# Matmul products beside two attentions, cut into runs of 12 and placed from tables; fewer transfers that clear the maxima rows

## The chip, the cores and the metric

One NeuronCore of a Trainium2 chip runs the whole program. The metric is the device time of one execution in microseconds, as the median of several runs. The engines work side by side, each through its own list of instructions in order: TensorE (PE, matmuls, with its weight loads shown as PEld), VectorE (DVE), ScalarE (ACT), GpSimd (POOL), and SyncE (SP), whose queue issues nearly all of the transfers. Engines wait for each other on semaphores.

## The reference, cut to what matters

Two transformer layers on `x` of shape (8, 1024, 256), 8 being the batch, all in float32.

```python
x = x + attn0(layernorm(x), Mq, Mk, Mv)         # 8 heads, softmax(q k^T / 8) over 1024 keys
x = x + fp4_ffn(layernorm(x), w_gate, w_up, w_down)   # blockwise FP4 quantized SwiGLU, 704 wide
x = x + attn1(layernorm(x), w_qkv, ...)          # 16 heads of 16, q and k normalised, softmax(q k^T)
x = x + moe_lora(layernorm(x), W, b, R, A, B)    # base product, top 2 of 8 experts, rank 16
```

Products with float16 operands are made three times over (high by high, high by low, low by high halves), so that the sum is as exact as float32 needs.

## The kernel before, in words

The work of a batch element (below: a batch) is done in tiles of 128 rows, 8 tiles a batch. Its two attentions have 64 steps each. A step of attention 0 (`attn0`) is one block of scores in `pS` (16 matmuls, L459, half of `pS` each), a maximum on DVE (L1239), an exponential of 1,024 columns on ACT (L914) with its row sums, a reciprocal of the sums on DVE (L1256), a scaling of the values on POOL (L1726), and the values' matmuls into `pV` (L560), some steps later. A step of attention 1 (`attn1`) is four score matmuls of 512 columns (L650), four exponentials of 512 columns (L953), and eight value matmuls (L690), one step later. Its scores take no maximum: two rows of the queries' operand that would carry maxima are filled with zeros. These are the maxima rows of the title. They get other contents only if a flag, computed from the data, asks for the general path.

Everything else is done beside these two attentions. The program has phases. In phase x of a period the steps of `attn1` for batch i-1 run beside the feed-forward part of batch i (`ffn`: gate and up products of 352 columns, down products of 256) and the first products of batch i+1 (`ln0`, `ln0_values`). In phase y the steps of `attn0` for batch i+1 run beside its later projections, the mixture part of batch i-1 (`moe_proj`, `moe_rt`, `moe`) and the heads of batch i (`heads_qkv`, `heads_T`). Batches 0 and 1 and the last batch have special cases at both ends of the program.

Which instruction follows which on an engine is fixed when the program is built. Each part is a generator (a lane) that yields a place, a number on a scale on which attention step n stands at n, and then issues its next piece. `weave` always lets the lane with the lowest place go on:

```python
while at:
    first = min(at, key=lambda x: x[:2])
    place = next(first[2], None)
```

Places come from small formulas, one set for all five engines, such as `ffn_at(t) = .5 + 6.75 * t` and `qkv_at(t)`, with fixed offsets per engine. A piece on PE is a whole product, or half of a long one: 24 matmuls of 352 columns for a gate or an up product, 36 of 256 for half of a down product, 48 of 256 for a projection (`project`) or for a pair of value tiles. `mm3` issues 12 matmuls at once: three combinations of halves, each as four matmuls on 32 of the 128 columns of weights.

```python
def mm3(dst, w, m, start=True, stop=True):
    by_columns(dst, w[0], m[0], start, False)
    by_columns(dst, w[0], m[1], False, False)
    return by_columns(dst, w[1], m[0], False, stop)
```

All these products share a ring of three banks, `pR`. `take` hands them out in turn, and waits on PE until the use before of the same bank has been read (`r_free`). `pS` and `pV` belong to the attentions.

The SP queue issues in its own woven order: `fill` (L1958), which copies the operands of `attn0`; `halves` (L1962), a transposing transfer of normalised rows; `put` (L2072), which writes the heads to a scratch tensor `scr`; and the transfers that read them back, keys (L2126) and queries (`queries`, L2155). Before the queries of a group of heads, `no_maxima` (L2141) clears the group's maxima rows with four transfers of 4 KB. In batches 0 to 6 that is done for two of four groups, so 8 transfers a batch, all between the keys and the transposing transfer `xT<-ua` of the next batch's `ffn_in`. The last batch clears 8 in `heads_end` and 8 more (L2141 to `x`) beside its attention.

Of the kernel before, what the change touches and what calls it, by code (L numbers as in the profile page):

```python
# [15 lines left out]
NB = 8  # L16
# [20 lines left out]
def placed(at, lane):  # L37

    for place in lane:
        yield at(place) if callable(at) else at + place  # L40

# [13 lines left out]
def build(nc, a, out):  # L55
    with ExitStack() as ctx:
# [155 lines left out]
        keys_late = sem("keys_late")  # L212
# [74 lines left out]
        P_AT = (2.1, 3.5, 6.5, 8.5)  # L287
        R_AT = (19.0, 21.6, 25.2, 27.0)

        def project_at(pair, n):  # L290
            return 16 * (pair - 1) + (0.0, 0, -1)[pair - 1] + 3.5 * n

        def qkv_at(t):
            return 11 + 9 * (t // 2) + 4 * (t % 2)


        def qkv_end(t):
            return .9 * t - .5

        def sums_end(tp):  # L300
            return qkv_end(2 * tp + 1) + 1.5

        def turn_end(tp):
            return 8 + 2 * tp + 2 * (tp // 2)
# [23 lines left out]
        def sums_at(tp):  # L328
            return 17.2 + 9 * tp

        def ffn_at(t):
            return .5 + 6.75 * t

        def ln_at(b, p):

            return 0.71 * p - 7.8 if b == 1 else p

        def v0_at(b, tp):
            return ln_at(b, 34.3 + 2.2 * tp) if b else 57 + tp

# [3 lines left out]

        def fin_at(n):


            return -23.0 + 0.9 * n if n < 20 else 3.3 + .8 * (n - 20)
# [10 lines left out]
        def at_step(p, to):  # L359

            of = (0, 10, 17.7, 19.5, 30, 39, 62)
            n = max(i for i in range(6) if p >= of[i])
            return to[n] + (p - of[n]) * (to[n + 1] - to[n]) / (of[n + 1] - of[n])
# [17 lines left out]
        def group_in(b, hg):  # L381

            return (fill1[hg % 2], fill1_at(b, hg)) if b + 1 < NB or hg < 2 else (fill1_end[hg % 2], 16 * 18)
# [35 lines left out]
        def fill1_at(b, hg):  # L419

            return 16 * (22 * b + 10 + 12 * (hg // 2))
# [14 lines left out]
        def _(e):  # L436
# [34 lines left out]
            def project(b, pair, w, jp):  # L471
                u = take(("qk0", b, pair, w, jp))
                e.wait_ge(tr_in["0"][pair // 2], 16 * (b + 1))
                if b == 1 and pair == 0:

                    e.wait_ge(tr_in["F"][1], 16)
                for h in range(2):
                    for k in range(2):
                        i = mm3(bank(u)[:, 256 * h:256 * h + 256],
# [3 lines left out]

            def ln0(b):
                if b == 0:
                    yield 20
                    e.wait_ge(const_in, 14)
                    e.wait_ge(m_in, 3)
                for n, (w, jp) in enumerate(((0, 0), (0, 2), (1, 0), (1, 2))):
                    yield ln_at(b, 43.4 + 4 * n)  # L490
                    project(b, 0, w, jp)

            def ln0_values(b):
                for tp in range(4):
                    yield v0_at(b, tp)
                    u = take(("v0", b, tp), two=False)
                    e.wait_ge(tr_in["0"][tp // 2], 16 * (b + 1))
                    for t in range(2):
                        for k in range(2):
                            i = mm3(bank(u)[:, 256 * t:256 * t + 256], columns_of(xT0, k, 2 * tp + t),  # L500
                                    parts(mv, k, slice(0, 256)), start=(k == 0), stop=(k == 1))
                    i.then_inc(r_full[u.bank], 1)

            def projections(b):
                for pair in range(1, 4):
                    for n, (w, jp) in enumerate(((0, 0), (0, 2), (1, 0), (1, 2))):
                        yield project_at(pair, n) + .3
                        project(b, pair, w, jp)

            def attn0(b):  # L510
                for n in range(69):
# [22 lines left out]
                    yield n + .2  # L534
                    if n > 4 and (n - 5) % 8 == 7:
                        outputs0(b, (n - 5) // 8)
# [4 lines left out]
            def outputs0(b, g):  # L541
                u = take(("o0T", b, g), two=False)
                e.wait_ge(o0_in, 8 * b + g + 1)
                for k in range(2):
                    i = transpose(bank(u)[:, 128 * k:128 * k + 128], oTa[:, 128 * k:128 * k + 128])
                i.then_inc(r_full[u.bank], 1)
# [17 lines left out]

            def ffn(b):
                def gate_up(t, hv, s_):
                    u = take(("gu", b, t, hv, s_), two=(s_ == 0))
                    e.wait_ge(tr_in["F"][t // 4], 16 * (b + 1))
                    for k in range(2):
                        i = mm3(bank(u)[:, 0:FH], columns_of(xT1, k, t),  # L570
# [3 lines left out]
                for t in range(NT + 1):  # L574
                    s = ffn_at(t)
                    if t < NT:
                        if b == 0 and t == 0:
                            yield s
                            freed(("w", len(jobs) - 1, 640))
                        for n in range(4):  # L580
                            yield s + 1.1 * n + .1
                            gate_up(t, n // 2, n % 2)
                    if t:
                        yield s + 4.5
                        u = take(("dn", b, t - 1), two=False)
                        e.wait_ge(trh_in[(t - 1) % 2], 16 * (4 * b + (t - 1) // 2 + 1))
                        for k in range(6):
                            if k == 3:
                                yield s + 5.6
# [4 lines left out]
            def general(b, hg):  # L594

                k = 4 * b + hg
                e.wait_ge(*group_in(b, hg))
                q, kk_ = operands(b, hg)
# [30 lines left out]
            def attn1(b):  # L629
                for n in range(67):  # L630
# [21 lines left out]
                    yield n + .2  # L652
                    if n > 2 and (n - 3) % 8 == 7:
                        outputs1(b, (n - 3) // 8)
# [3 lines left out]

            def outputs_end():

                for k in range(2):
                    yield (56.3, 66.9)[k]
# [7 lines left out]
            def outputs1(b, k):  # L670
# [1581 lines left out]
```

## Time and profile before

| What | Before |
|---|---|
| Time, median of 3 runs | 2958.23 us (2956.24 to 2965.4) |
| Span of the profiled execution | 2954.7 us |
| Busy in the span: PE, DVE, ACT, POOL | 87%, 71%, 67%, 40% |
| Mean granted TensorE clock | 0.969 of full speed |
| From one batch to the next, middle of the run | some 340 us |

The profiled execution has no time of its own in the results beside its span. The span runs from the first to the last instruction; the median of the timed runs is 3.5 us above it. The page tells busy shares, and they are means over stages with different limits, so the stages have to be looked at one by one.

### The profile page before, as it was taken

The page shows a single profiled execution, that of the slowest core. Times are in us where ns is not written, and L with a number is a line of the kernel's source. Part 1 is how long each engine was busy: PE and PEld are TensorE (multiplying, and loading weights), DVE is VectorE, ACT ScalarE, POOL GpSimd, SP SyncE. Part 2 cuts the span into 40 slices and gives each one's busy share as a digit, 9 for nine tenths or more (in the row PEclk, how much of TensorE's full clock was granted, in tenths as well). Part 3 has the DMA queues.
Part 4 walks back from the last instruction along what each step waited for, and adds up shares of the span by engine and source line. Part 5 has one row for each costly group of instructions (what it writes and reads, how often), then busy time and mean ns, then how long its engine had stood idle before and what let it go on. Part 6 is the DMA issues. An engine that isn't in the chain of part 4 may idle for free.

```text
span 2954.7 us, 115301 instructions
## 1 busy us (share of the span) xinstructions
PE 2580.8 (87%) x50178; PEld 1403.9 (48%) x50178; DVE 2104.1 (71%) x4266; ACT 1979.9 (67%) x3763; POOL 1193.4 (40%) x1677
## 2 busy tenths in 40 slices
PE   4766786998989989999889989899889999899697
PEld 3434554445644466444554456444654446444233
DVE  6778766866778488875879578775788667775433
ACT  3541255876668866787668866787668776687684
POOL 3563156215642167223653156322662256411210
PEclk9997999999999999999999999999999999999798
DMA  4212332234424252323424253243423253222310
GB/s 127 44 38 46 67 84 69 50 49 86 97 64 81 47 111 62 77 51 73 109 63 75 34 108 79 58 78 58 103 70 66 49 86 84 63 67 47 87 31 16
DMA packets 470460, 203.52 MB, mean 69 GB/s; under 512 B 283289, under 2 KB 459937, under 8 KB 469929
## 3 DMA queue, kind: packets, MB, share of 16 engines
q1 hardware_dynamic: 467960, 194.07, 31.9%
q8 instruction: 413, 6.77, 0.9%
q10 hardware_dynamic: 1968, 1.72, 0.2%
q14 instruction: 119, 0.97, 0.1%
HBM read 46.48 MB, written 32.51 MB: 27 GB/s over the span
## 4 chain that ended last, share of the span: by engine, by line
PE 42%; DVE 29%; ACT 8%; SPq 7%; issue 7%; DMA 5%; POOL 2%; DVEq 0%; ACTq 0%; POOLq 0%
PE pR L459 18%; PE pV L690 9%; DVE nmaxa L1239 8%; PE pS L459 5%; PE pS L650 5%; ACT ub L953 5%; PE pV L560 3%; SPq L1958 2%; PE pR L469 2%; SPq L2155 2%; SPq L2141 1%; DMA xT<-ua 1%; DMA xT<-xhb 1%; DVE ua L1142 1%; DVE ua L1119 1%
## 5 line engine op out<-in xcount | busy, mean ns | idle before, releaser
L953 ACT ACTIVATE ub<-pS 128x512 f32<-128x512 f32 x2048 | 1048.2, 612 | 227.6 <-PE pS L650 227.0
L1239 DVE TENSOR_REDUCE nmaxa<-pS 128x1 f32<-128x1024 f32 x512 | 621.1, 1214 | 249.9 <-PE pS L459 247.2
L914 ACT ACTIVATE ua<-pS,nmaxa 128x1024 f32<-128x1024 f32 x384 | 427.9, 1114 | 406.1 <-DVE nmaxa L1239 403.9
L459 PE MATMUL pS<-ua 128*32 128x512 f16 x8192 | 544.1, 387 | 102.2 <-ACT ua L914 77.4
L690 PE MATMUL pV<-ub,vaug 128*17 128x512 f32 x4096 | 536.7, 597 | 14.6 <-DVE ub L1397 13.2
L1726 POOL TENSOR_TENSOR ua<-ua,rz 128x256 f32<-128x256 f32 x512 | 332.0, 650 | 429.4 <-DVE rz L1256 414.4
L650 PE MATMUL pS<-ub 50*128 50x512 f16 x1920 | 352.0, 386 | 27.6 <-DMA ub<-scr 11.6
L459 PEld LDWEIGHTS pS<-ua 128*32 128x32 f16 x8192 | 210.1, 98 | 273.9 <-ACT ua L914 110.4
L459 PE MATMUL pR<-wgu,xT 128*32 128x352 f16 x6144 | 284.9, 321 | 49.5 <-DMA xT<-ua 24.6
L650 PEld LDWEIGHTS pS<-ub 50*128 50x128 f16 x1920 | 96.5, 93 | 404.4 <-ACT ub L953 334.6
L560 PE MATMUL pV<-ua 128*32 128x128 f32 x6144 | 244.7, 279 | 22.6 <-DVE oTa L1250 12.2
L459 PEld LDWEIGHTS pR<-wgu,xT 128*32 128x32 f16 x6144 | 160.9, 99 | 188.1 <-issue 114.6
L914 ACT ACTIVATE EA<-pS,nmaxa 128x1024 f32<-128x1024 f32 x128 | 142.6, 1114 | 137.1 <-DVE nmaxa L1239 135.9
L560 PEld LDWEIGHTS pV<-ua 128*32 128x32 f32 x6144 | 169.3, 112 | 92.3 <-DVE oTa L1250 25.8
L459 PE MATMUL pR<-wqkv,xT 128*32 128x512 f16 (+1 forms) x3072 | 147.4, 330 | 13.8 <-DMA xT<-xhb 10.2
L1790 POOL CAST xhb<-at_ 128x256 f16<-128x256 f32 x56 | 24.1, 431 | 301.9 <-DVE at_ L1389 253.4
L1771 POOL TENSOR_TENSOR EA<-ua,EA 128x704 f16<-128x704 f32 x28 | 45.5, 1627 | 239.4 <-DVE EA L1348 239.4
L690 PEld LDWEIGHTS pV<-ub,vaug 128*17 128x17 f32 x4096 | 84.7, 96 | 114.4 <-issue 73.9
L459 PE MATMUL pR<-wd,ua 128*32 128x256 f16 x4032 | 130.5, 273 | 3.3 <-DVE ua L1307 1.9
L459 PEld LDWEIGHTS pR<-wd,ua 128*32 128x32 f16 x4032 | 103.9, 97 | 56.5 <-issue 47.9
L459 PE MATMUL pR<-xT,mq 128*32 128x256 f16 x3072 | 98.4, 279 | 26.2 <-DMA xT<-ua 25.2
L1297 DVE SCALAR_TENSOR_TENSOR ua<-ua,pR 128x352 f32<-128x352 f32 x112 | 57.5, 513 | 89.4 <-ACT ua L924 89.4
(262 smaller groups left out, 4062.6 us busy)
## 6 DMA issues: line engine op xcount, KB each, us to landing
ua<-ua SPq DMA_DIRECT2D x384, 128.0 KB, 2.7
ub<-scr SPq DMA_DIRECT2D x264, 64.0 KB, 2.9
scr<-ub SPq DMA_DIRECT2D x30, 512.0 KB, 3.8
x<-in_L_attn_x SPq DMA_DIRECT2D x8, 1024.0 KB, 6.2
between<-x SPq DMA_DIRECT2D x7, 1024.0 KB, 5.0
ub<-between SPq DMA_DIRECT2D x7, 1024.0 KB, 5.9
out<-ub SPq DMA_DIRECT2D x7, 1024.0 KB, 5.4
ub<-scr SPq DMA_DIRECT2D x192, 32.0 KB, 1.8
```

Source lines behind the costliest of these rows:

```text
L459: i = e.matmul(dst[j:j + 32], w[:, j:j + 32], m, start=start, stop=stop)
L469: return e.matmul(dst, src, ident[0:n, 0:n], is_transpose=True)
L560: i = e.matmul(pV[32 * jl:32 * jl + 32, 128 * jg:128 * jg + 128], vs[n % 4][:, j, :], EA[n % 4][:, 128 * j:128 * j + 128], start=(c == 0 a ...
L650: e.matmul(pS[:, 512 * hl:512 * hl + 512], kk_[row:row + 50, o, 128 * c:128 * c + 128], q[row:row + 50, o, 512 * qh:512 * qh + 512]).then_ ...
L690: i = e.matmul(pV[32 * hl:32 * hl + 17, :], vaug[:, c, 4 * hg + hl, :], EB[(4 * n + hl) % 8], start=(c == 0), stop=(c == 7))
L914: e.activation(EA[n % 4], pS[:, 1024 * (n % 2):1024 * (n % 2) + 1024], ACT.Exp, bias=nmaxa[:, n % 32:n % 32 + 1], accum_out=zz[:, n % 8:n ...
L953: e.activation(EB[(4 * n + hl) % 8], pS[:, 512 * hl:512 * hl + 512], ACT.Exp).then_inc(e1_in, 1)
L1239: e.tensor_reduce(nmaxa[:, n % 32:n % 32 + 1], pS[:, 1024 * (n % 2):1024 * (n % 2) + 1024], AXX, ALU.max, negate=True).then_inc(max0_in, 1)
L1297: e.scalar_tensor_tensor(ht[hv][:, FH:2 * FH], ht[hv][:, 0:FH], 1.0, bank(g)[:, 0:FH], ALU.add, ALU.mult).then_inc(r_free[g.bank], 1)
L1726: e.tensor_tensor(vs[m % 4], vv[:, :, 32 * c:32 * c + 32], rz[:, c:c + 1].unsqueeze(2).to_broadcast([128, 8, 32]), ALU.mult).then_inc(vs_i ...
L1958: e.dma_start(dst[r0:r0 + 64, par::2, o:o + 256], sh[64 * par:64 * par + 64, w, l, :, :]).then_inc(fill0[pair % 2], 16)
L2155: e.dma_start(dst[at:at + 16, o:o + 2, :], scr[b % 2, w_, l, 64 * hg:64 * hg + 64, :].rearrange("(h p d) n -> p d h n", p=2, d=16)[par]).t ...
```

## The change

There are two parts. First, all the formulas for places are gone, and each lane yields places from a table of its own, by engine and lane, in some cases by batch. A piece on PE is now one `mm3`, 12 matmuls (24 for the 136-column products), and each has its own entry. `take` and the waits for operands stand in front of the first piece of a product, the signal behind the last. The places of attention steps stay whole numbers. The reciprocals and outputs of `attn0`, the transposes and the normalising of outputs of both attentions, which were fixed to steps, have become lanes with tables (`sums0`, `outputs0`, `outputs1`). Which work is done is unchanged.

```diff
+PLACES = {
...
+    ('PE', 'ln0_values'): (35.155, 35.155, 35.155, 35.155, 40.121, 40.121, 40.121, 40.121, 40.121, 40.121, 40.121, 40.121, 40.121, 40.121, 40.121, 40.121),
...
+    ('PE', 'ffn'): (1.303, 1.303, 1.975, 1.975, 2.941, 2.941, 4.367, 4.367, 5.189, 6.711, 8.164, 8.164, 9.355, 9.629, 10.68, 10.68, 11.401, 12.102,
...
+    ('PE', 'heads_T'): (23.635, 24.955, 33.712, 33.712, 41.849, 41.849, 51.575, 51.575),
...
+def timed(engine):
+    def of(lane):
+        def at(*args):
+            keys = [(engine, lane.__name__, *args[:n]) for n in range(len(args), -1, -1)]
+            places = next((PLACES[k] for k in keys if k in PLACES), ())
+            for _, place in zip(lane(*args), places, strict=True):
+                yield place
...
+            @timed("PE")
             def ffn(b):
                 def gate_up(t, hv, s_):
-                    u = take(("gu", b, t, hv, s_), two=(s_ == 0))
-                    e.wait_ge(tr_in["F"][t // 4], 16 * (b + 1))
                     for k in range(2):
+                        yield
+                        if k == 0:
+                            u = take(("gu", b, t, hv, s_), two=(s_ == 0))
+                            e.wait_ge(tr_in["F"][t // 4], 16 * (b + 1))
                         i = mm3(bank(u)[:, 0:FH], columns_of(xT1, k, t),
...
-                        for n in range(4):
-                            yield s + 1.1 * n + .1
-                            gate_up(t, n // 2, n % 2)
+                        for n in range(4):
+                            yield from gate_up(t, n // 2, n % 2)
```

Second, `no_maxima` clears the rows of all four heads' places with two transfers of 16 KB, once a batch instead of twice. They count on a semaphore of their own, for which the first group of heads waits. The last batch makes two such calls, one in `heads_end` and one beside its attention.

```diff
             def no_maxima(b, hg):
-                o = 2 * (hg % 2)
-                for par in range(2):
-                    for c in range(2):
-                        at = 64 * par + 48 + c
-                        e.dma_start(operands(b, hg)[0][at:at + 1, o:o + 2, :].rearrange("a h (c n) -> a (h c) n", n=128),
-                                    wd[64:80, 0, 5, 0:128]).then_inc(group_in(b, hg)[0], 16)
+                for at in (48, 112):
+                    e.dma_start(operands(b, hg)[0][at:at + 2, :, :].rearrange("a h (c n) -> a (h c) n", n=256),
+                                wd[64:66, 0, 5, :].unsqueeze(1).to_broadcast([2, 16, 256])).then_inc(zeros_end if hg else zeros_in, 16)
...
+                no_maxima(b, 0)
                 for hg in range(2):
                     queries(b, hg)
```

## Rows read from the trace of the kernel before

**Rows 1.** The page: busy time by engine, then the chain that ended last by engine.

```profile
PE 2580.8 (87%) x50178; PEld 1403.9 (48%) x50178; DVE 2104.1 (71%) x4266; ACT 1979.9 (67%) x3763; POOL 1193.4 (40%) x1677
...
PE 42%; DVE 29%; ACT 8%; SPq 7%; issue 7%; DMA 5%; POOL 2%; DVEq 0%; ACTq 0%; POOLq 0%
```

**Rows 2.** Windows by stage: stretch, length, busy per engine, PEclk, DMA, GB/s.

```profile
55.00:245.00 190.00, 137.06 (x2772) 80.89 (x2772) 142.65 (x321) 92.40 (x188) 107.99 (x139) 0.90 0.19 41
...
310.00:520.00 210.00, 159.28 (x3566) 104.12 (x3570) 145.13 (x250) 103.86 (x177) 105.75 (x163) 0.91 0.31 70
...
860.00:1035.00 175.00, 168.57 (x2618) 72.99 (x2618) 115.45 (x219) 141.85 (x282) 35.27 (x35) 0.99 0.31 56
1035.00:1199.00 164.00, 144.18 (x3642) 97.79 (x3638) 136.96 (x286) 103.87 (x185) 111.59 (x173) 0.99 0.41 92
...
2740.00:2955.00 215.00, 170.93 (x2200) 70.53 (x2198) 82.82 (x272) 144.19 (x284) 29.59 (x40) 0.87 0.18 46
```

**Rows 3.** Timeline of the SP queue at the turn from y to x.

```profile
836.89 2.71 SPq L2126 DMA_DIRECT2D ub<-scr  x6
839.64 3.21 SPq L2141 DMA_DIRECT2D ub<-wd  x4
842.89 2.91 SPq L2155 DMA_DIRECT2D ub<-scr  x6
845.85 3.24 SPq L2141 DMA_DIRECT2D ub<-wd  x4
849.14 2.91 SPq L2155 DMA_DIRECT2D ub<-scr  x6
852.15 2.87 SPq L1962 DMA_TRANSPOSE xT<-ua  x1
```

**Rows 4.** Timelines of POOL, SP and PE at two other turns, and at this one.

```profile
847.30 2.14 POOL L1759 TENSOR_TENSOR ua<-xhb,ua 128x1024 f16<-128x1024 f32 x1
...
857.69 1.08 PE L459 MATMUL pR<-wgu,xT 128*32 128x352 f16 x24 [3.11 <-DMA xT<-ua]
...
2206.08 2.14 POOL L1759 TENSOR_TENSOR ua<-xhb,ua 128x1024 f16<-128x1024 f32 x1
...
2212.87 1.84 SPq L1962 DMA_TRANSPOSE xT<-ua  x1
...
2217.37 1.95 PE L459 MATMUL pR<-wgu,xT 128*32 128x352 f16 x24 [4.00 <-DMA xT<-ua]
...
2544.97 2.14 POOL L1759 TENSOR_TENSOR ua<-xhb,ua 128x1024 f16<-128x1024 f32 x1
...
2549.67 2.23 SPq L1962 DMA_TRANSPOSE xT<-ua  x1
```

**Rows 5.** Timelines of DVE, SP, PE and ACT in the last batch.

```profile
2777.57 3.07 SPq L2141 DMA_DIRECT2D x<-wd  x4
...
2788.79 2.45 SPq L2141 DMA_DIRECT2D x<-wd  x4
...
2794.62 0.69 DVE L1516 TENSOR_TENSOR xhb<-ua,xhb 128x512 f16<-128x512 f32 x1
...
2800.07 4.54 SPq L1962 DMA_TRANSPOSE xT<-xhb  x2
2804.63 1.55 PE L459 MATMUL pR<-wmoe,xT 128*32 128x136 f16 x48 [6.40 <-DMA xT<-xhb]
```

**Rows 6.** Timelines of ACT and PE in phase x: start, length, operation, idle before.

```profile
940.23 2.06 ACT L953 ACTIVATE ub<-pS 128x512 f32<-128x512 f32 x4 [0.44 <-PE pS L650]
942.73 2.07 ACT L953 ACTIVATE ub<-pS 128x512 f32<-128x512 f32 x4 [0.44 <-PE pS L650]
...
952.69 0.61 PE L650 MATMUL pS<-ub 50*128 50x512 f16 x4
953.17 2.06 ACT L953 ACTIVATE ub<-pS 128x512 f32<-128x512 f32 x4 [1.05 <-PE pS L650]
953.23 1.49 PE L459 MATMUL pR<-mv,xT 128*32 128x256 f16 x48
954.55 1.07 PE L459 MATMUL pR<-wgu,xT 128*32 128x352 f16 x24
956.89 2.06 ACT L953 ACTIVATE ub<-pS 128x512 f32<-128x512 f32 x4 [0.76 <-PE pS L650]
...
1020.64 9.90 ACT L953 ACTIVATE ub<-pS 128x512 f32<-128x512 f32 x20 [1.03 <-PE pS L650]
...
1024.06 1.04 PE L650 MATMUL pS<-ub 50*128 50x512 f16 x4
```

**Rows 7.** Timeline of PE, SP and ACT at the turn from x to y.

```profile
1019.05 1.17 PE L459 MATMUL pR<-wd,ua 128*32 128x256 f16 x36
...
1020.26 8.05 SPq L1958 DMA_DIRECT2D ua<-ua  x12
...
1031.08 1.05 PE L459 MATMUL pS<-ua 128*32 128x512 f16 x16 [1.07 <-DMA ua<-ua]
```

**Rows 8.** DMA issues over the whole span: KB each, median us to landing.

```profile
ub<-scr SPq DMA_DIRECT2D x264, 64.0 KB, 2.9
...
ub<-wd SPq DMA_DIRECT2D x64, 4.0 KB, 1.7
```

**Rows 9.** Waits over the whole span: total, times, longest.

```profile
ACT ua L914 <- DVE nmaxa L1239: 403.9, 323, 9.3
...
ACT ub L953 <- PE pS L650: 227.0, 330, 9.3
...
DVE small L1377 <- PE pR L469: 103.4, 41, 4.4
...
ACT ua L924 <- PE pR L459: 26.8, 14, 5.9
...
PEld pR L469 <- POOL ub L1849: 18.6, 10, 4.6
```

More of the change, by code:

```diff
@@ L539, in attn0, with outputs0 @@
                         values0(b, n - 3)
[L541 to L546, printed above, removed]
+            @timed("PE")
+            def outputs0(b):
+                for g in range(8):
+                    yield
+                    u = take(("o0T", b, g), two=False)
+                    e.wait_ge(o0_in, 8 * b + g + 1)
+                    for k in range(2):
+                        i = transpose(bank(u)[:, 128 * k:128 * k + 128], oTa[:, 128 * k:128 * k + 128])
+                    i.then_inc(r_full[u.bank], 1)
             def values0(b, n):
@@ L668, in outputs_end, with outputs1 @@
                     i.then_inc(r_full[u.bank], 1)
-            def outputs1(b, k):
-                u = take(("oT", b, k), two=False)
-                e.wait_ge(o1_in, 8 * b + k + 1)
-                for t in range(4):
-                    i = transpose(bank(u)[:, 128 * t:128 * t + 128], oTb[:, 512 * (k % 2) + 128 * t:512 * (k % 2) + 128 * t + 128])
-                i.then_inc(r_full[u.bank], 1)
+            @timed("PE")
+            def outputs1(b):
+                for k in range(8):
+                    yield
+                    u = take(("oT", b, k), two=False)
+                    e.wait_ge(o1_in, 8 * b + k + 1)
+                    for t in range(4):
+                        i = transpose(bank(u)[:, 128 * t:128 * t + 128], oTb[:, 512 * (k % 2) + 128 * t:512 * (k % 2) + 128 * t + 128])
+                    i.then_inc(r_full[u.bank], 1)
             def values1(b, n):
@@ L1226, in projections @@
                     for n, (w, jp) in enumerate(((0, 0), (0, 2), (1, 0), (1, 2))):
-                        yield project_at(pair, n) + 1.1
+                        yield
                         project(b, pair, w, jp)
             def attn0(b):
-                def outputs(g):
+                for n in range(64):
+                    yield n
+                    e.wait_ge(s0_in, 64 * b + n + 1)
+                    e.tensor_reduce(nmaxa[:, n % 32:n % 32 + 1], pS[:, 1024 * (n % 2):1024 * (n % 2) + 1024], AXX, ALU.max,
+                                    negate=True).then_inc(max0_in, 1)
@@ new lines, in sums0, with outputs0 @@
+            @timed("DVE")
+            def sums0(b):
+                for n in range(64):
+                    yield
+                    c = n % 8
+                    e.wait_ge(e0_in, 64 * b + n + 1)
+                    e.reciprocal(rz[:, c:c + 1], zz[:, c:c + 1]).then_inc(rz_in, 1)
+            @timed("DVE")
+            def outputs0(b):
+                for g in range(8):
+                    yield
+                    e.wait_ge(pv0_in, 64 * b + 8 * g + 8)
+                    if g:
+                        full(("o0T", b, g - 1))
+                    e.tensor_copy(oTa[:, :], pV[:, 0:256]).then_inc(o0_in, 1)
+                    yield
@@ L1258, in ffn_in @@
+            @timed("DVE")
             def ffn_in(b):
@@ L1365, in attn1, with outputs1 @@
             def attn1(b):
-                for n in range(67):
-                    hg = group_at(b, n // 8)[0]
-                    if n < 64 and n == group_step(b, hg):
-                        yield n - .1
-                        general(b, hg)
-                    yield n + .3
-                    if n > 2 and (n - 3) % 8 == 7:
+                for hg in range(4):
+                    yield group_step(b, hg) - .1
+                    general(b, hg)
+            @timed("DVE")
+            def outputs1(b):
+                for n in range(8, 67):
+                    if n > 8 and (n - 3) % 8 == 7:
+                        yield
                         k = (n - 3) // 8
@@ L1705, in _, with spread @@
             e.memset(wd[:, :, 5, :], 0.0).then_inc(const_in, 1)
-            def spread(s, b, at):
-                yield at
+            @timed("POOL")
+            def spread(s, b):
+                yield
                 e.wait_ge(stat_in[s], 16 * b + 16)
@@ L2029, in ln0 @@
                     fill(b, 0, w)
+            @timed("SP")
             def projections(b):
```

617 lines of the change are left out of this document (368 added, 249 removed), and 81 rows, old and new, of the table PLACES.

## The prediction

> **What bounds the kernel now.** I read the page first, for the shares and the chain [rows 1], then the busy time in windows cut at the turns between the phases [rows 2], then the timelines of those turns and of some steps, and last the waits [rows 9]. No engine is full: PE is shown busy 87% of the span. The chain that ended last is 42% PE and 29% DVE, and 7% SP's queue: transfers being issued one after another. The windows say where the time lies. A phase x takes 175 us and a phase y 164 us, seven pairs of them from 520 to 2740 us. The start (two stretches of 190 and 210 us) and the last 215 us are looser: PE is busy 72 to 80% there.
>
> In phase x PE looks full, 168.6 of 175 us. It is not. Four score matmuls are 0.61 us long at 952.69 and 1.04 us at 1024.06 [rows 6]: at the second place PE waits inside them for the exponentials. The Trainium skill says so too (Trainium Kernel Development and Optimization, Performance Expectations: matmul busy time is a bad metric, because matmuls are pipelined), and these two rows agree; no number below needs it. The reader is to see the step, start to start of four exponentials. A step with no product beside it takes 9.90 / 5 = 1.98 us, ACT's pace. With half a down product (36 matmuls) it takes 942.73 - 940.23 = 2.50 us. With a value product and a gate or up product (48 + 24) it takes 956.89 - 953.17 = 3.72 us. At the full clock (2.4 GHz; PEclk is 0.99 over phase x) four matmuls side by side stream their columns at once, so a run of 12 is an estimated 3 x 256 / 2400 = 0.32 us, or 0.44 us with 352 columns. Then 2.50 - 0.96 = 1.54 and 3.72 - 1.28 - 0.88 = 1.56 us are left for the attention's own matmuls. So a step is the longer of 1.98 us and 1.54 us plus its products, and a step loses time on PE only where less than 0.44 us of products stands in it.
>
> **Part 1, the transfers.** At the turn from y to x the SP queue issues 6 key transfers, 4 that clear, 6 queries, 4 that clear, 6 queries, then the transposing transfer on which the next batch's first gate product waits [rows 3]. The 8 clears take 3.21 + 3.24 = 6.45 us. The new ones are 2; each copies between buffers on the chip as L2141 and L1958 do, 0.6 to 0.7 us of queue each [rows 3, 7], so 1.3 us. The queue reaches the transposing transfer 5.1 us sooner. Its data are late next: POOL's L1759 ends at 847.30 + 2.14 = 849.44, 2.71 us before the issue at 852.15 [rows 3, 4]. PE sat idle 3.11 us for it. Over seven turns the delay between L1759 and the issue is 2.56 us (2544.97 + 2.14 to 2549.67) to 4.65 us (2206.08 + 2.14 to 2212.87), and PE's idle time 2.7 to 5.95 us (three of the seven are in [rows 4]). The smaller of the two, turn by turn, sums to 22.8 us. I take 22; bounds are 7 x 2.5 = 17 and 7 x 4.65 = 33 us.
>
> What hides the new clears' landing: 4 KB land in 1.7 us and 64 KB in 2.9 [rows 8]; these are 16 KB, issued ahead of 12 queries which take 5.8 us of queue and whose landing the same group waits for anyway. Bounds for landing are 1.7 us and, were they slower than the slowest case so far, some 6 us; both are inside 5.8 + 2.9. I cost it at nothing; without the cover it would be up to 6 us a turn. The Trainium skill has a rule that speaks against this form (DMA: Bandwidth & Descriptors, Why a DMA increments its semaphore by 16 and not by 1): a transfer is spread over at most as many engines as divide its slowest dimension, here 2 rows instead of 16. By it the two engines carry 8 KB each, where a clear of 4 KB had 256 B for each; no row here has such a transfer. By the rule as by the rows the sum keeps its 22 us, as long as the landing stays under the 8.7 us.
>
> In the last batch 8 clears beside the attention take 3.07 + 2.45 = 5.52 us, and behind them stands the transposing transfer for the router, issued at 2800.07 though its data end at 2794.62 + 0.69 = 2795.31 [rows 5]. PE waits 6.40 us for it. Two clears are left: 5.5 - 1.3 = 4.2 us sooner, under the 4.8 us that the data allow. I take 4.
>
> **Part 2, the order on PE.** I merged the places of both versions for a middle batch by `weave`'s rule and summed the products between one attention step and the next. Phase x holds 52.9 us of products in both. Before, 15 of 64 steps have less than 0.44 us of them; after, 12. With the step rule, phase x is 158.0 us before and 156.1 after: 1.9 us a batch. The new order is not even. Between steps 38 and 39 stand half a down product and three of the four value products, 15 runs, 4.8 us (three value products share the place 40.121; before, the four stood at 34.3, 36.5, 38.7 and 40.9). That costs PE nothing more than three lumps of 2.2 us do, since PE is the slower engine in all of them, though ACT idles 4.3 us at a stretch. The measured phase is 175 us against my 158, so 17 us are waits for data that this sum does not see.
>
> Phase y by the same count, with a floor of 2.0 and 1.45 us for the attention's own matmuls (an estimate: 16 of 512 columns and 16 float32 of 128, and the windows' 164 us [rows 2]), goes from 155.6 to 154.6: 1.0 us a batch. In all 7 x 2.9 = 20 us. Bounds: 0, if data waits eat it, and 7 x 17 = 119 us if the tables removed every wait in phase x.
>
> At the turn from x to y the last down product ends at 1020.2, twelve copies take SP 8.05 us, and the first scores wait for them, 1.07 us of idle PE [rows 7]. The new table has all but one run of that product before values 56, a step earlier than its second half was. So up to 1.07 us a turn; I take 0.4, 3 us in all.
>
> What is moved against waits: PE waited 18.6 us in weight loads for POOL's normalising of the heads, and DVE 103.4 us for transposes of outputs [rows 9]. The tables put `heads_T` 0.4 to 1.7 places later, and two to four pieces more before DVE's `outputs1` in the first half of phase x. DVE's wait is on the path only where DVE is nearly full. I take nothing for it, nor for the 615 us of start and end; PE is idle 53, 51 and 44 us in the three stretches [rows 2], and as bounds I take a quarter of these 148 us won, 37, and an eighth lost, 18.
>
> **Sum.** 22 + 4 + 20 + 3 = 49 us less. The profiled span is 2954.7 us; 2905.7 after. The median lies 3.5 us above the span, and I keep that: 2909 us.
>
> **The rivals.** (a) The tables remove data waits too. They place DVE's and POOL's pieces one by one, and PE, DVE and ACT all idle at the start. If a third of the 17 us goes in each phase x, and 20 us at the start and end, that is 7 x 5.7 + 20 = 60 more: 2850. Against it: the lump at step 38, and similar ones in the tables of batch 0 (18 runs at 15.698, 18 at 34.875).
> (b) The order gives nothing and the queue does: 2958 - 26 = 2932.
> (c) No change: the transposing transfer comes sooner, but the first gate product then runs where the attention's last steps ran, and all of it comes back as a later wait: 2958 within 9 us.
> (d) Slower, by one mechanism: a product cut in pieces holds its bank over an attention step. In the new order 23 products of a middle batch are spread over two or more steps, against 8 before. The ring has three banks handed out strictly in turn, so the reader of a bank is one step late and stands in ACT's or DVE's queue in front of the attention's own work; such a wait of ACT for a product is 26.8 / 14 = 1.9 us each now [rows 9]. At 15 more splits a batch and seven batches, 0.47 us each gives back the whole 49 us; beyond 0.55 us it is slower by more than 0.3%. At 0.8 us it costs 84: 2993. Against it: 14 of the 23 are gate, up or down products, and the eight down products were spread over two steps before as well.
>
> **How the numbers follow.** The forecast, 2890 to 2928, has 0.42; (a), below 2890, 0.20; (b), 2928 to 2949, 0.11; (c) 0.08; (d) 0.19. A measurement here can tell about 0.3% (9 us) from no change. Faster is 0.42 + 0.20 + 0.11 = 0.73, same 0.08, slower 0.19. The range reaches from (a)'s far side, 2860, to 2985 inside (d); below and above it lie about 0.1 each.
>
> **What would show it.** Right: L2141 twice a batch; L1962 issued within 0.5 us of L1759's end; PE idle under 1 us before the first gate product; steps without products as before at 1.98 us; a gap of some 4 us in ACT's exponentials near step 38. Wrong: new waits of PE for `zeros`, ACT or DVE waiting longer than 2 us each for `pR`, a phase y over 164 us, or a start (to 520 us) that moves by more than 20 us either way, which my sum leaves out.

## Result, and the profile after

The changed kernel takes 2792.7 us (2790.7 to 2793.7), the kernel before 2961.1 us beside it: a ratio of 0.9439, 95% interval 0.9422 to 0.9456. It is 5.6% faster. I had forecast 2909 us and a range of 2860 to 2985; the time lies below the whole range.

The page of the changed kernel, beside [rows 1]: busy time by engine, then the chain that ended last.

```profile
PE 2545.9 (91%) x50178; PEld 1408.6 (50%) x50178; DVE 2067.0 (74%) x4266; ACT 1979.6 (71%) x3763; POOL 1203.5 (43%) x1677
...
PE 48%; DVE 19%; issue 8%; ACT 8%; DMA 8%; SPq 5%; POOL 4%; DVEq 0%; POOLq 0%; ACTq 0%
```

PE, DVE, ACT and POOL execute as many instructions as before. What fell is DVE's share of the chain, from 29% to 19%. The span fell by 163.8 us. To see where, I cut both traces at the first and last exponential of each attention. The first attention 1 starts at 479 instead of 521 us (42). The six phases y that follow take 154.4 us each instead of 163.7 (56), and the seven phases x 162.9 instead of 167.8 (34). The six turns from y to x among them take 9 us instead of 23 (14), the six from x to y 10 instead of 16 (6). The last attention 1 takes 146.1 instead of 157.0 (11), what follows it 35 instead of 37 (2), and what stands before it is 1 us longer. That adds up to 164.

Windows by stage of the changed kernel, as in [rows 2] (the third is a phase x, the fourth a phase y):

```profile
48.00:209.00 161.00, 126.18 (x2664) 75.58 (x2660) 132.42 (x292) 90.87 (x186) 105.17 (x134) 0.95 0.23 49
298.00:479.00 181.00, 149.59 (x3526) 99.64 (x3518) 142.98 (x245) 102.77 (x178) 104.66 (x163) 0.97 0.35 80
803.00:962.00 159.00, 157.05 (x2463) 68.49 (x2454) 111.13 (x218) 136.08 (x272) 35.60 (x35) 1.00 0.29 60
963.00:1125.00 162.00, 150.61 (x3774) 103.37 (x3767) 136.34 (x287) 107.67 (x192) 112.90 (x173) 0.98 0.40 90
2605.00:2791.00 186.00, 163.12 (x2118) 62.76 (x2108) 71.57 (x252) 133.51 (x270) 25.84 (x38) 0.95 0.18 43
```

The turn from y to x, which answers to [rows 3, 4]: timeline of SP, POOL and PE of the changed kernel.

```profile
785.29 1.48 SPq L2377 DMA_DIRECT2D ub<-wd  x2
786.81 6.79 SPq L2389 DMA_DIRECT2D ub<-scr  x12
789.81 2.15 POOL L1978 TENSOR_TENSOR ua<-xhb,ua 128x1024 f16<-128x1024 f32 x1
793.70 2.87 SPq L2189 DMA_TRANSPOSE xT<-ua  x1
...
798.71 1.08 PE L624 MATMUL pR<-wgu,xT 128*32 128x352 f16 x24 [1.23 <-DMA xT<-ua]
```

The two clears take 1.48 us where eight took 6.45. POOL ends at 791.96 and the transposing transfer is issued 1.74 us later, still behind the queries: the queue is later than the data here too, though by less than the 2.56 to 4.65 us before. PE's idle time went from 3.11 to 1.23 us. At the turn from x to y, which answers to [rows 7], ACT goes from its last exponentials of attention 1 to the first of attention 0 after 1.63 us instead of 2.90, and PE's first scores, at 962.95, no longer wait for the copies:

```profile
951.65 12.02 ACT L1140 ACTIVATE ub<-pS 128x512 f32<-128x512 f32 x24 [1.35 <-PE pS L823]
965.29 1.11 ACT L1100 ACTIVATE ua<-pS,nmaxa 128x1024 f32<-128x1024 f32 x1 [1.63 <-DVE nmaxa L1434]
...
962.95 1.04 PE L624 MATMUL pS<-ua 128*32 128x512 f16 x16
```

In the last batch [rows 5] the wait of 6.40 us is gone:

```profile
2622.80 1.34 SPq L2377 DMA_DIRECT2D x<-wd  x2
...
2641.01 5.64 SPq L2189 DMA_TRANSPOSE xT<-xhb  x2
...
2647.70 0.89 PE L624 MATMUL pR<-wmoe,xT 128*32 128x136 f16 x48
```

The list of waits of the changed kernel, beside [rows 9] (L1100 answers to L914, L1140 to L953, L1579 to L1377; ACT's waits at L1111 for `ua` and PE's for POOL's normalising are below the listed ones):

```profile
ACT ua L1100 <- DVE nmaxa L1434: 283.3, 262, 8.4
DVE nmaxa L1434 <- PE pS L624: 167.0, 169, 9.5
ACT ub L1140 <- PE pS L823: 164.9, 270, 4.7
...
DVE small L1579 <- PE pR L634: 52.0, 28, 4.3
```

ACT waited 403.9 us for DVE's maxima and now 283.3. That is the loop of attention 0: PE makes scores, DVE their maximum, ACT the exponentials, PE the values. For attention 1's scores ACT waited 227.0 us and now 164.9. DVE's wait for transposed outputs halved. PE's value products of attention 1 waited 13.2 us for DVE to read earlier values (L1397) and now 0.7. My sum had taken nothing for any of them.

### The profile page after: what moved, and what is told of

It is laid out like the page before. It is cut to its first block, busy times and chain, and to the rows that moved or that the text cites. A ratio compares the mean times of both kernels' runs of the same rounds, so it can differ in the third digit from the quotient of the medians.

```text
span 2790.9 us, 115256 instructions
## 1 busy us (share of the span) xinstructions
PE 2545.9 (91%) x50178; PEld 1408.6 (50%) x50178; DVE 2067.0 (74%) x4266; ACT 1979.6 (71%) x3763; POOL 1203.5 (43%) x1677
## 4 chain that ended last, share of the span: by engine, by line
PE 48%; DVE 19%; issue 8%; ACT 8%; DMA 8%; SPq 5%; POOL 4%; DVEq 0%; POOLq 0%; ACTq 0%
PE pR L624 19%; PE pV L864 11%; PE pS L823 7%; PE pS L624 7%; DVE nmaxa L1434 6%; ACT ub L1140 5%; PE pV L729 3%; SPq L2185 2%; PE pR L634 2%; DMA scr<-ub 2%; DMA xT<-xhb 2%; DMA xT<-ua 1%; DMA ua<-EA 1%; SPq L2389 1%; DMA ua<-ua 1%
## 5 line engine op out<-in xcount | busy, mean ns | idle before, releaser
L1140 ACT ACTIVATE ub<-pS 128x512 f32<-128x512 f32 x2048 | 1049.8, 610 | 168.5 <-PE pS L823 164.9
L1100 ACT ACTIVATE ua<-pS,nmaxa 128x1024 f32<-128x1024 f32 x384 | 427.6, 1114 | 286.9 <-DVE nmaxa L1434 283.3
L624 PE MATMUL pS<-ua 128*32 128x512 f16 x8192 | 550.4, 387 | 69.3 <-ACT ua L1100 41.3
L823 PE MATMUL pS<-ub 50*128 50x512 f16 x1920 | 342.5, 385 | 9.0 <-ACT ub L1140 1.6
L624 PE MATMUL pR<-wgu,xT 128*32 128x352 f16 x6144 | 283.9, 317 | 33.6 <-DVE x L1331 14.1
L1100 ACT ACTIVATE EA<-pS,nmaxa 128x1024 f32<-128x1024 f32 x128 | 142.6, 1114 | 84.9 <-DVE nmaxa L1434 84.8
L1991 POOL TENSOR_TENSOR ua<-ua 128x704 f16<-128x704 f32 x28 | 42.9, 1532 | 265.4 <-DVE ua L1548 265.4
L1048 ACT ACTIVATE ua<-pR 128x512 f16<-128x512 f32 x128 | 76.5, 605 | 68.5 <-PE pR L624 66.6
L1317 DVE SCALAR_TENSOR_TENSOR ua<-pR,ua 128x512 f16<-128x512 f32 x128 | 86.7, 683 | 50.6 <-ACT ua L1048 49.4
```

What stands on the lines that cost most here:

```text
L624: i = e.matmul(dst[j:j + 32], w[:, j:j + 32], m, start=start, stop=stop)
L823: e.matmul(pS[:, 512 * hl:512 * hl + 512], kk_[row:row + 50, o, 128 * c:128 * c + 128], q[row:row + 50, o, 512 * qh:512 * qh + 512]).then_ ...
L1048: e.activation(dst, view(bank(u)), ACT.Copy, scale=scale).then_inc(r_mid[u.bank], 1)
L1100: e.activation(EA[n % 4], pS[:, 1024 * (n % 2):1024 * (n % 2) + 1024], ACT.Exp, bias=nmaxa[:, n % 32:n % 32 + 1], accum_out=zz[:, n % 8:n ...
L1140: e.activation(EB[(4 * n + hl) % 8], pS[:, 512 * hl:512 * hl + 512], ACT.Exp).then_inc(e1_in, 1)
L1317: e.scalar_tensor_tensor(dst, view(bank(u)), scale, hi, ALU.mult, ALU.subtract).then_inc(r_free[u.bank], 1)
```

## Experiments

Every kernel below holds work, sums and buffers of the full one; only places, and where said the clears, differ. "Phase y" is the mean of the six middle ones from first to last exponential of attention 0, "phase x" that of the six beside them for attention 1, each from its run's one trace. Runs beside one another (e1 to e4, e5 to e8, e9 to e12) shared a chip and the kernel before, whose median was 2958.5, 2956.3 and 2963.7. So between these groups a few microseconds say nothing, and the ratios compare better. Times in the text are medians. The excerpts of edits are against the changed kernel. The expectations give phase x as 165 us with the old tables and 158 with the new: my reading of its end was some microseconds early. From first to last exponential it is 169.7 (e1) and 163.5 (e4), as in the table.

| kernel | us | ratio to before | first attention 1 at | phase y | phase x |
|---|---|---|---|---|---|
| before | 2961.1 | 1 | 521 | 163.7 | 169.3 |
| changed | 2792.7 | 0.944 | 479 | 154.4 | 163.9 |
| e1 transfers alone | 2935.7 | 0.991 | 518 | 163.8 | 169.7 |
| e2 tables alone | 2835.5 | 0.958 | 487 | 154.4 | 164.2 |
| e3 whole products | 2813.4 | 0.951 | 478 | 155.9 | 165.7 |
| e4 tables, middle only | 2838.3 | 0.959 | 515 | 154.6 | 163.5 |
| e5 middle, lanes of x | 2908.5 | 0.984 | 513 | 166.6 | 164.0 |
| e6 middle, lanes of y | 2877.5 | 0.973 | 520 | 155.8 | 169.6 |
| e7 middle, PE+ACT+DVE | 2889.5 | 0.978 | 516 | 157.9 | 169.6 |
| e8 middle, POOL+SP | 2937.0 | 0.993 | 521 | 164.9 | 169.5 |
| e9 middle, all but SP | 2874.2 | 0.970 | 516 | 155.2 | 169.3 |
| e10 middle, all but POOL | 2859.9 | 0.966 | 514 | 157.8 | 163.8 |
| e11 start only | 2898.6 | 0.978 | 484 | 163.9 | 169.5 |
| e12 values spread | 2801.7 | 0.947 | 481 | 153.7 | 165.7 |

**e1, the transfers alone.** The new clears with every place by the old rules, on all engines:

```diff
-    ('PE', 'projections'): (1.437, 1.437, 1.437, 1.437, 4.272, 4.272, 4.272, 4.272, ...
+    ('PE', 'projections', 3): (0.3, 0.3, 0.3, 0.3, 3.8, 3.8, 3.8, 3.8, ...
-    ('SP', 'ln0'): (30.779, 35.832, 59.701),
+    ('SP', 'ln0', 3): (31.4, 33.6, 59.5),
...
```

> The order on PE, DVE, ACT and POOL is that of the kernel before, instruction by instruction; only the clearing of the maxima rows is the new one (2 transfers a batch). Theory of the prediction: the transposing transfer is late at seven turns and in the last batch, so 22 + 4 = 26 us go, 2935 us (0.991 of before). Rival: the data or another wait are late right behind it, and less than 9 us go. A second rival, that the queue is what the whole change is about, would give over 100 us.

2935.7 us, ratio 0.991 (0.9886 to 0.9934), 22.8 us less than before's 2958.5. The turns from y to x fell from 3 to 7 us to 0 to 2 us, 24 us over seven, and the transposing transfer is issued 0.03 to 0.08 us after POOL's end at each of them. The last attention 1 fell from 157.0 to 152.9 us. So the queue's term of my sum, 26 us, stands, and the other 143 us are the tables' or come with them.

**e2, the tables alone.** The new places with the old eight clears:

```diff
-                for at in (48, 112):
-                    e.dma_start(operands(b, hg)[0][at:at + 2, :, :].rearrange("a h (c n) -> a (h c) n", n=256),
+                for par in range(2):
+                    for c in range(2):
+                        at = 64 * par + 48 + c
+                        e.dma_start(operands(b, hg)[0][at:at + 1, o:o + 2, :].rearrange("a h (c n) -> a (h c) n", n=128),
...
```

> The tables and runs of 12 are in, the maxima rows are cleared by 8 transfers a batch as before. If queue and tables add up, the transposing transfer is 2.5 to 4.6 us late again at each turn, and this is 20 to 33 us slower than the changed kernel (2815 to 2826 us). If the new order hides the queue (steps of attention 0 can run on while it is busy), it is within 9 us of the changed kernel.

2835.5 us, 0.958 (0.9515 to 0.964), slower than either theory had it. Beside the changed kernel the transfers are worth 43 us, beside the old order 23. The turns say why: with the new tables and the old clears the seven take 5.5 to 7.4 us each, where they took 3 to 7 with the old tables and 0 to 4 in the changed kernel; they hold 36 of the 44 us between the two traces. Attention 0 had become shorter, and the transposing transfer is issued 4.3 to 7.4 us after POOL's end, against 2.6 to 4.7 in the kernel before. The same queue cost more beside the shorter attention.

**e3, products whole.** The new tables, but all runs of one product go at the place of its first:

```diff
-    ('PE', 'moe_proj'): (3.278, 3.278, 3.278, 3.278, 3.278, 3.278, 4.165, 4.165, 6.795, 6.795, 6.795, 6.795, 7.12, 9.801, 10.154, 10.154),
+    ('PE', 'moe_proj', 3): (3.278, 3.278, 3.278, 3.278, 3.278, 3.278, 3.278, 3.278, 6.795, 6.795, 6.795, 6.795, 7.12, 7.12, 7.12, 7.12),
```

> The tables are in, but the runs of 12 of one product (of one half of a down product) stand together at the place of its first run, as in the kernel before. Theory of the order (what counts is which product stands at which step on which engine, so that nobody waits): within 15 us of the changed kernel, 2780 to 2808 us. Theory of the runs (the size of a piece is what pays, since scores wait for at most one run): most of the gain goes, over 2870 us.

2813.4 us, 0.951 (0.9451 to 0.9575), 5 us above the first theory's range and far from the second's. Its four times, 2808 to 2823, lie above all of the changed kernel's; the intervals of the ratios just touch. Runs of 12 are worth some 21 us of 143, with the readers' places kept as they are for split products. The splitting that the change is named for is the small part, and it gains: whatever a split product costs by holding its bank, rival (d), is less than what splitting gains.

**e4, the tables in the middle only.** New places for the six middle pairs of phases, old ones before and after; new clears. Beside the changed kernel, for instance:

```diff
-    ('PE', 'ln0_values', 1): (17.331, 19.588, 19.588, ...
+    ('PE', 'ln0_values', 1): (16.553, 16.553, 16.553, 16.553, ...
...
```

> New transfers everywhere, new tables only in the phases 1 to 6 of the run's middle; start (prologue, batches 0 and 1 up to attention 0) and end keep the old places. From the spans of the phases: the changed kernel is 42 us shorter up to the first attention 1, and 9 to 14 us at the end; so about 110 to 120 us of the 168 should be in here, 2840 to 2850 us. If the prediction's sum by evenness were right for the middle, it would be 26 + 20: 2912 us.

2838.3 us, 0.959 (0.9529 to 0.965): 97 us under e1, where the same step of my sum had 20. Both phases gain, y 9.2 and x 6.2 us. Rival (a) was right in kind; it had 60 us for the middle.

**e5 and e6, by phase.** The same, but only the lanes that run beside attention 1 (e5) or beside attention 0 (e6) are new:

```diff
 e5
-    ('ACT', 'moe_rt'): (19.01, 22.61, 25.672, 28.771),
+    ('ACT', 'moe_rt', 3): (19.85, 22.45, 26.05, 27.85),
...
 e6
-    ('ACT', 'ln0_values'): (35.547, 40.303, 40.303, 41.016),
+    ('ACT', 'ln0_values', 3): (34.4, 36.6, 38.8, 41.0),
...
```

> New transfers; of the middle tables (worth 97 us over the transfers alone, 2935.7 to 2838.3) only those of the lanes that belong to phase x: feed-forward, its input, the first products of the next batch, the outputs of attention 1. Theory of separate stages: attention 1 shrinks from 165 to 158 us, six times 7 us, and attention 0 stays at 164: 2894 us, plus or minus 8. Rival: the two sets only work together, since they share three banks and each engine's list; then the sum of this and the next run falls short of 97 us by more than 15.

> The same with the lanes of phase y alone: projections, mixture, heads, reciprocals and outputs of attention 0. Theory of separate stages: attention 0 shrinks from 164 to 155 us six times: 2882 us, plus or minus 8. Rival as in the run before.

e5 2908.5 us (0.984, 0.9813 to 0.9868), above its expected range; e6 2877.5 (0.9726, 0.9699 to 0.9754), within it. They are 27 and 58 us under e1, 85 of 97 together; by the ratios 21 and 54, 75 of 95. So whether the sum falls short by more than 15 us is not clear. The phases say more. e6 shortens phase y to 155.8 us and leaves phase x as it was. e5 shortens phase x to 164.0 us, but phase y grows from 163.8 to 166.6: the lanes of phase x, moved alone, cost something in the other phase; why was not shown. Phase y, where I had put 1 us a batch, is the larger part.

**e7 and e8, by engine.** New middle tables on PE, ACT and DVE alone (e7) or on POOL and SP alone (e8):

```diff
 e7
-    ('SP', 'heads_store'): (18.828, 22.101),
+    ('SP', 'heads_store', 3): (21.6, 25),
...
 e8
-    ('DVE', 'heads_norm'): (17.149, 26.877, 35.401, 44.423),
+    ('DVE', 'heads_norm', 3): (17.2, 26.2, 35.2, 44.2),
...
```

> New transfers, middle tables on PE, ACT and DVE, old places on POOL and SP. Theory that the order of products and of their readers is what pays: nearly all of the 97 us, 2838 to 2850 us. Rival: POOL's in-order work (the scaled values that each step of attention 0 needs stand behind long pieces of normalising) and SP's are half of it: 2885 us. The old places of POOL may also wait for what now comes later, and cost more than they did.

> The complement: middle tables on POOL and SP alone. Theory of the products: within 10 us of the transfers alone (2926 to 2946). Rival: 2890 us or less.

e7 2889.5 us (0.9778, 0.9754 to 0.9802): 46 of the 97, and none of it in phase x, which is as long as with the old tables. e8 2937.0 (0.9933, 0.9912 to 0.9954): nothing against e1, and yet it is what e7 lacks: POOL's and SP's places bring 51 us, but only beside the new places of the other three.

**e9 and e10, SP and POOL apart.** The middle tables on all engines but SP (e9) and on all but POOL (e10), for instance:

```diff
 e9
-    ('SP', 'ln0'): (30.779, 35.832, 59.701),
+    ('SP', 'ln0', 3): (31.4, 33.6, 59.5),
 e10
-    ('POOL', 'ln0'): (35.202, 35.202, 35.202, 35.202),
+    ('POOL', 'ln0', 3): (30.2, 30.6, 32.4, 32.8),
```

> New tables for the six middle phases on PE, ACT, DVE and POOL; SP keeps its old places there. New transfers; start and end old. The same tables with SP's too gave 2838, with neither POOL's nor SP's 2890; so 51 us hang on the two together. Theory P: POOL's places carry it (it multiplies the value halves, halves the feed-forward's rests and normalises the heads, all of it just ahead of a product): 2838 within 9 here. Theory S: SP's places carry it (its transfers bring the operands of the next phase): about 2890 here. Theory B: each needs the other, both runs of this pair lie near 2865 to 2890.

> The counterpart: new tables for the middle on PE, ACT, DVE and SP, POOL with its old places. Theory P: 2890 within 9. Theory S: 2838. Theory B: 2865 to 2890.

e9 2874.2 us (0.9701, 0.9683 to 0.9719), e10 2859.9 (0.9659, 0.9643 to 0.9675): 36 and 22 us above e4, 33 and 20 by the ratios. Neither P nor S. The times lie near theory B's, but its reason, that each needs the other, does not hold: the two parts add up to some 51 us, and they do different things. Without SP's places phase x is 169.3 us instead of 163.5, as long as with the old tables, and phase y hardly moves; without POOL's phase y is 157.8 instead of 154.6 and phase x stays. What POOL's places do shows in the waits of e4 and then of e10 for the scaled values that POOL makes in each step of attention 0; the difference is 15 us of the 20:

```profile
PE pV L1025 <- POOL ua L2239: 11.3, 12, 3.4
```

```profile
PE pV L1025 <- POOL ua L2239: 26.7, 33, 2.8
```

What SP's places do can be seen too. Timelines of e9, SP and POOL, and PE, in one phase x (L2485 transposes half of the next batch's input, L2685 the operands of two head groups, L2506 the feed-forward's hidden values):

```profile
926.03 1.04 POOL L2248 CAST ua<-ua 128x1024 f16<-128x1024 f32 x1 [5.06 <-DVE ua L1636]
927.15 2.15 POOL L2251 TENSOR_TENSOR ua<-ua 128x1024 f16<-128x1024 f32 x1
929.40 1.95 SPq L2485 DMA_TRANSPOSE xT<-ua  x1
931.39 7.64 SPq L2685 DMA_DIRECT2D ub<-scr  x12
931.69 1.53 POOL L2287 TENSOR_TENSOR ua<-ua 128x704 f16<-128x704 f32 x1 [2.39 <-DVE ua L1844]
939.14 1.29 SPq L2506 DMA_TRANSPOSE ua<-ua  x1
942.94 2.11 PE L920 MATMUL pR<-wd,ua 128*32 128x256 f16 x36 [4.18 <-DMA ua<-ua]
```

The same stretch of e4, SP only:

```profile
915.17 8.09 SPq L2685 DMA_DIRECT2D ub<-scr  x12
923.36 1.80 SPq L2485 DMA_TRANSPOSE xT<-ua  x1
925.63 1.52 SPq L2506 DMA_TRANSPOSE ua<-ua  x1
```

In e9 SP has both halves of the input, places 31.4 and 33.6, ahead of the twelve transfers. POOL stood 5.06 us for DVE's rows (L1636) of the second half and ends at 927.15 + 2.15 = 929.30. SP stands until 929.40; the twelve stand behind it, and behind them the hidden values, complete at 933.22 and issued at 939.14. PE stands 4.18 us for them. It happens once in each of the six phases x, 2.91 to 4.68 us, 23 us in all; e4 shows one such wait, of 0.21 us. The rest of the 36 us was not traced to a wait. In e4 the second half has place 35.8, and the twelve go while the second half is still being made. It is not POOL's new places that make it late: e7 has POOL's old ones and shows the same chain (twelve copies, hidden values issued 6.09 us after POOL's end at 936.48, wait of PE), 23.1 us in six phases x:

```profile
934.65 7.81 SPq L2685 DMA_DIRECT2D ub<-scr  x12
942.57 1.29 SPq L2506 DMA_TRANSPOSE ua<-ua  x1
946.35 2.11 PE L920 MATMUL pR<-wd,ua 128*32 128x256 f16 x36 [4.19 <-DMA ua<-ua]
```

The Trainium skill states the mechanism (DMA: Bandwidth & Descriptors, Anatomy of one DMA: the DMA engines don't wait on semaphores, the wait happens on the issuing sequencer before dispatch), and e9's trace agrees: 5.92 us from complete to issued.

So the tables' places are no list of single improvements. Here SP's old order cost nothing beside the old places of the others and 36 us beside the new ones.

**e11, the start only.** New places up to the first attention 1; old after, for instance:

```diff
-    ('DVE', 'heads_norm'): (17.149, 26.877, 35.401, 44.423),
+    ('DVE', 'heads_norm', 3): (17.2, 26.2, 35.2, 44.2),
...
```

> New tables for the start alone (the lanes of the preparation and of the first three stretches, up to the first attention 1), new transfers, all later places old. In the full kernel the first attention 1 begins 39 us sooner than with the old tables. Theory: that gain is made in the start itself and kept: 2935.7 - 39 = 2897 within 8. Rival: the start is sped up only because what follows takes work off it, then 2920 or more.

2898.6 us, 0.9783 (0.9767 to 0.98): 37 us under e1, and the first attention 1 starts at 484 us instead of 518. The start's gain is made there and kept. I had counted nothing for it, with 37 as the upper bound for start and end together.

**e12, value products spread.** The full kernel, with the four value products of phase x back at four places:

```diff
-    ('PE', 'ln0_values'): (35.155, 35.155, 35.155, 35.155, 40.121, 40.121, 40.121, 40.121, 40.121, 40.121, 40.121, 40.121, 40.121, 40.121, 40.121, 40.121),
+    ('PE', 'ln0_values', 3): (34.3, 34.3, 34.3, 34.3, 36.5, 36.5, 36.5, 36.5, 38.7, 38.7, 38.7, 38.7, 40.9, 40.9, 40.9, 40.9),
```

> The full new kernel, but in the six middle phases x the four value products go back to one by one at their old places (34.3, 36.5, 38.7, 40.9), with ACT's reads behind them, where the new table puts three of them at one place. My evenness theory: the lump of 4.8 us of products between two steps idles ACT some 4 us and DVE too; spread out it gains 0 to 2 us in each phase x: 2781 to 2793. Rival: the lump costs nothing, since readers and banks are arranged around it, and the spread products collide with the down products near steps 34 to 41: 2793 to 2805.

2801.7 us, 0.9467 (0.9447 to 0.9488): not faster, and by the medians 9 us slower. Phase x is 165.7 us instead of 163.9, which is 11 us over six. The lump is there in the changed kernel as I forecast: 144 matmuls in 4.10 us, and the exponentials stop for 4.35 us. Removing it does not pay. The intervals touch, so I only conclude that a more even PE brings nothing. No version was found that beats the changed kernel.

**Where phase y gains.** Timelines of one stretch of e1 (old places), PE and ACT:

```profile
1069.99 1.05 PE L920 MATMUL pS<-ua 128*32 128x512 f16 x16 [0.18 <-ACT ua L1396]
1070.87 0.61 PE L1025 MATMUL pV<-EA,ua 128*32 128x128 f32 x16
1073.31 1.05 PE L920 MATMUL pS<-ua 128*32 128x512 f16 x16 [1.84 <-ACT ua L1396]
...
1069.84 0.61 ACT L1472 CAST xhb<-ub 128x512 f16<-128x512 f32 x1
1070.35 0.60 ACT L1344 ACTIVATE ua<-pR 128x512 f16<-128x512 f32 x1
1070.84 1.05 ACT L1512 ACTIVATE ub<-ub 128x1024 f32<-128x1024 f32 x1
1071.78 0.38 ACT L1500 ACTIVATE vaug<-pR 128x256 f32<-128x256 f32 x1
1072.05 1.12 ACT L1396 ACTIVATE ua<-pS,nmaxa 128x1024 f32<-128x1024 f32 x1
```

ACT puts four pieces between two exponentials, 2.3 us, in a step in which PE has no product at all; PE stands 1.84 us. It does so in each of the six phases y, 1.84 us each time, and the kernel before in each of its six, 1.83 us. The two engines' loads fall in different steps. Now the changed kernel, where ACT does the same two long pieces (L1216, L1048):

```profile
1006.83 1.05 ACT L1216 ACTIVATE ub<-ub 128x1024 f32<-128x1024 f32 x1
1007.77 0.59 ACT L1048 ACTIVATE ua<-pR 128x512 f16<-128x512 f32 x1
1008.28 1.11 ACT L1100 ACTIVATE ua<-pS,nmaxa 128x1024 f32<-128x1024 f32 x1
...
1008.06 2.12 PE L624 MATMUL pR<-wqkv,xT 128*32 128x256 f16 x48
1010.01 0.61 PE L729 MATMUL pV<-EA,ua 128*32 128x128 f32 x16
1010.45 1.04 PE L624 MATMUL pS<-ua 128*32 128x512 f16 x16
```

PE has its 48 matmuls in that very step, and no idle time before the next scores. Over the whole span PE's wait for these exponentials went from 77.4 us in 95 places to 41.3 in 62. All idle time of PE inside the six phases y, summed from the traces, is 109.6 us in e1, 58.1 in e4 and 54.4 in the changed kernel, and 48.7, 19.5 and 18.8 of it stand before scores that wait for an exponential. So the 56 us by which the six phases y got shorter are PE's waits, some 30 of them of this kind. Inside the six phases x it fell from 28.2 to 9.2 us, half of what they gained. That a step's loads have to match is my reading of these lines; no run set one step right alone.

## Why the prediction was wrong

**Part 1 was right for the old order.** 26 us forecast, 22.8 measured (e1). The seven turns gave 24 us where I took 22 (the smaller of delay and idle time, turn by turn, sums to 22.1 in the trace, not to 22.8), and the last attention 4 where I took 4; the seven phases x, 0.7 us longer each in e1, took 5 back. What I missed is that the term depends on the rest: 43 us with the new tables.

**Part 2 failed, and it is the step "I merged the places of both versions for a middle batch".** It counted products on PE per attention step and so priced the tables at 20 us. The middle tables are worth 97 us (e4). The count itself comes out of the traces much the same: 14 steps of a phase x with less than 0.44 us of products before, 11 after, which by my step rule is 2.1 us. It was blind in three ways. It took a constant floor for the attention's own work in phase y, 2.0 us, and with it no wait of PE for ACT or DVE; from that phase came 1.0 us in my sum and 9.3 in the trace, where PE's idle time fell by as much. In phase x it found "17 us are waits for data that this sum does not see" and then took nothing of them. They were some 11: 175 us is the window from 860 to 1035, with the turn in it, and from first to last exponential the six phases x average 169.3 against my 158. 5 to 6 a batch went. And it didn't merge SP's and POOL's places, which are worth 51 us beside the others (e7 to e10).

**"I take nothing for it, nor for the 615 us of start and end"** cost 37 us at the start (e11), the whole of my upper bound for start and end. What e1, e4 and e11 leave of the full gain, 2935.7 - 97 - 37 - 2792.7 = some 9 us, is mostly the end: the last attention 1 takes 151.6 us in e4, 152.7 in e11 and 146.1 in the changed kernel.

**The turn from x to y** I had at 3 us gained. Six of them went from 15.4 us in e1 to 9.8 in e4, 5.6 gained, inside my bound of 1.07 us a turn.

**The rivals.** (a) had a third of phase x's data waits, none of phase y's, and 20 us at start and end: 2850. In kind it was right, and its mechanism deserved the forecast's place; ACT's longest wait, for DVE's maxima with 403.9 us [rows 9], was the sign for it, and I had put that row down without pricing it. (b) says in its number what the transfers alone give, 2935.7 against 2932 (e1), but the order gave far more than nothing. (c) is refuted by e1; (d) by the whole and, for the splitting, by e3.

**The signs.** The clears came twice a batch, steps without products stayed at 12.02 / 6 = 2.00 us, and the gap in ACT's exponentials came, 4.35 us. The start moved by 42 us, which I had named as what would make the prediction wrong. L2189 was not issued within 0.5 us of its data, but 1.74 us after; with the old tables (e1) it was.

**What is open.** Which lanes carry phase y's gain: e6 shows only that they do it together. What the other half of phase x's gain is, which does not show as idle time of PE while ACT's wait for its scores fell by 62 us, was not shown. Whether the feed-forward's transposing transfers are all that SP's places are worth, and what the gating's and the feed-forward's lanes are worth alone, was not measured: the kernels made for these three questions gave no time. A table for one of PE, ACT or DVE alone couldn't be tried either: the three share the banks' ring, so their orders must agree.

## What to carry to other kernels

Where several in-order engines serve one loop, count the load of every engine in each step; here an even load on the busiest engine alone foretold 20 us where 97 came. A row of waits that runs to hundreds of microseconds along the loop belongs in the range, even where no single step of it can be priced; the largest here shrank by 121 us. Move a piece on one queue only together with the queue that waits for it, and let an in-order queue do what is ready ahead of what waits.

## What the hardware showed that I had not expected

The granted clock came out differently with another order of the same work. Windows over the same 100 us near the start, e1 first, then the changed kernel (columns as in [rows 2]):

```profile
60.00:160.00 100.00, 81.56 (x1782) 49.83 (x1778) 73.41 (x165) 54.83 (x108) 58.24 (x86) 0.92 0.26 57
```

```profile
60.00:160.00 100.00, 81.88 (x1884) 50.66 (x1877) 86.35 (x190) 58.98 (x116) 67.89 (x94) 1.00 0.30 65
```

PE is busy as long, but the second grants 2.4 GHz throughout, where the first spends part of the stretch at 1.2 GHz (0.92), and does 6% more matmuls. Up to the first attention 1 the granted clock is 0.89 in e1 and 0.93 in the changed kernel and in e11. Part of the start's 37 us may be this; how large a part, no run told apart. The last stretch, where PE's wait of 6.40 us went, rose from 0.87 to 0.95 [rows 2]. And a busy PE is no measure here: its share rose from 87% to 91% while its busy time fell by 35 us for the same 50178 matmuls. Part of the 35 us can be waits inside matmuls, 0.61 against 1.04 us for the same four [rows 6]; part is the clock, whose mean over the span rose from 0.969 to 0.977, an estimated 183 and 128 us at 1.2 GHz. The two were not told apart. The Trainium skill calls matmul busy time a bad metric, because matmuls are pipelined (Trainium Kernel Development and Optimization, Performance Expectations), and here the trace agrees that it misleads.
